# Steady attention chunks: the choice of the experts ahead of layer 2's first recurrence in VectorE's order

## The reference, cut to what matters

```python
def _time_mix_layer(x, ln_w, ln_b, Wk, Wv, Wr, Wo):
    normed = _layer_norm(x, ln_w, ln_b)
    k = einsum(normed, Wk); v = einsum(normed, Wv); r = sigmoid(einsum(normed, Wr))
    kv = k * v
    state = 0.95 * state + 0.05 * kv_t        # a scan over time
    return x + einsum(r * states, Wo)
x = layernorm(x + two_layers(x))
gate_out = einsum(x, Wg)
top_v, top_i = top_k(gate_out, 2)
probs = softmax(top_v)
out = sum over e of expert_e(x) * sum(probs * (top_i == e))
x = layernorm(x + out)
```

## Time and profile before

| | |
|---|---|
| median of 3 runs | 1275.16 us (1272.74 to 1279.75) |
| the profiled execution | 1267.26 us, its span 1265.5 us |
| TensorE busy | 1106.2 us, 87% of the span |
| DVE busy | 926.1 us, 73% |
| POOL busy | 869.1 us, 69% |
| ACT busy | 658.4 us, 52% |
| mean granted TensorE clock | 0.953 |

### The profile page before, as it was taken

The page is one execution under the profiler, slowest core; times in us unless marked ns, Lnnn a source line. Parts: engine busy times, 40 slices in busy tenths (PEclk is TensorE's granted clock), DMA queues, the critical chain, the costliest instruction groups (busy, mean ns, idle before and its releaser), DMA issues. The chain is left out here.

```text
span 1265.5 us, 23767 instructions
## 1 busy us (share of the span) xinstructions
PE 1106.2 (87%) x7172; PEld 990.4 (78%) x7172; DVE 926.1 (73%) x1973; ACT 658.4 (52%) x1091; POOL 869.1 (69%) x696
## 2 busy tenths in 40 slices
PE   7899888888888988738999999999999999999910
PEld 6777777777677777636888888888899999999910
DVE  6687888878887888746766666666667888888737
ACT  4455455555555444425544554445555666666618
POOL 3455777777877777667567776667667777777634
PEclk9999999999999999959999999999999999999965
DMA  3011111111111010237556665566669898888659
GB/s 150 17 51 67 43 43 52 51 50 50 50 50 39 31 48 34 67 102 196 146 148 161 158 153 142 140 155 159 148 156 229 240 228 247 227 244 227 141 165 384
DMA packets 80662, 164.20 MB, mean 130 GB/s; under 512 B 27424, under 2 KB 45600, under 8 KB 80352
## 3 DMA queue, kind: packets, MB, share of 16 engines
q1 hardware_dynamic: 49248, 126.16, 31.6%
q0 software_dynamic: 31360, 37.38, 15.7%
HBM read 118.01 MB, written 45.49 MB: 129 GB/s over the span
## 5 line engine op out<-in xcount | busy, mean ns | idle before, releaser
L1163 POOL DMA_INDIRECT x_acc<-fy_sb,pair_out x142 | 285.5, 2011 | 149.0 <-DVE fy_sb L1264 80.2
L1319 PE MATMUL fring<-fxh,fw_hi 128*128 128x256 f32 (+1 forms) x816 | 264.9, 325 | 3.6 <-DVE fxl L1255 1.9
L1321 PE MATMUL fring<-fxh,fw_lo 128*128 128x256 f32 (+1 forms) x816 | 265.4, 325 | 0.0
L1320 PE MATMUL fring<-fxl,fw_hi 128*128 128x256 f32 (+1 forms) x816 | 264.9, 325 | 0.0
L1182 ACT ACTIVATE fw_hi<-w_raw 128x1024 fp32r<-128x1024 f32 x153 | 161.1, 1054 | 150.0 <-PE fy L1362 138.7
L1235 DVE TENSOR_TENSOR fw_lo<-w_raw,fw_hi 128x1024 fp32r<-128x1024 f32 x153 | 186.5, 1219 | 17.9 <-ACT fw_hi L1182 17.0
L88 POOL DMA_INDIRECT xg<-x_src,pair_in x142 | 159.0, 1120 | 43.3 <-issue 42.7
L78 POOL DMA_INDIRECT slot_list<-pairs,slot_u x128 | 148.3, 1159 | 47.3 <-issue 30.5
L1319 PEld LDWEIGHTS fring<-fxh,fw_hi 128*128 128x128 f32 x816 | 153.7, 188 | 17.2 <-issue 2.3
L1320 PEld LDWEIGHTS fring<-fxl,fw_hi 128*128 128x128 f32 x816 | 153.7, 188 | 13.4
L1321 PEld LDWEIGHTS fring<-fxh,fw_lo 128*128 128x128 f32 x816 | 153.8, 188 | 13.2
(11 more groups left out here) (148 smaller groups left out, 2330.0 us busy)
## 6 DMA issues: line engine op xcount, KB each, us to landing
w_raw<-w_ffn SPq DMA_DIRECT2D x153, 512.0 KB
x_in<-h SPq DMA_DIRECT2D x16, 512.0 KB, 3.3
x_src<-x SPq DMA_DIRECT2D x16, 512.0 KB
x_acc<-x SPq DMA_DIRECT2D x16, 512.0 KB
acc<-x_acc SPq DMA_DIRECT2D x16, 512.0 KB, 7.6
out<-o SPq DMA_DIRECT2D x16, 512.0 KB, 6.6
xg<-x_src,pair_in POOLq DMA_INDIRECT x142
x_acc<-fy_sb,pair_out POOLq DMA_INDIRECT x142
```

The costliest lines, as they stand in the source:

```text
L1163: nc.gpsimd.indirect_dma_start(x_acc, bass.IndirectOffsetOnAxis(pair_out[j][:, q, 0:1].bitcast(U32), 0), y[j][:, q, :], None, compute_op=A ...
L1319: nc.tensor.matmul(out, hi, rows_hi, start=dc == 0, stop=False)
L1320: nc.tensor.matmul(out, hi, rows_lo, start=False, stop=False)
L1321: last = nc.tensor.matmul(out, lo, rows_hi, start=False, stop=dc == DC - 1)
```

## The change

On DVE, `choose(s - 3)` is now issued ahead of `recur(1, s - 1, 0)` in every step but s = 16 (`CHUNKS`), which keeps its own order. In steps 1 and 2 there is no choice yet, and in 17 and 18 no layer 2, so the order differs in steps 3 to 15. No other engine's code is touched.

```diff
                         recur(1, s - 1, e, j)
                         gated(dve, 1, s - 1, e)
                         y_lo(dve, 1, s - 1, e)
-                elif layer2:
-                    recur(1, s - 1, 0, j)
                 if within(s, 3, CHUNKS + 2) and not at(s, CHUNKS):
                     choose(s - 3)
+                if layer2 and not at(s, CHUNKS):
+                    recur(1, s - 1, 0, j)
                 if within(s, 1, CHUNKS - 2):
                     x_lo(0, s + 1)
                 if within(s, 3, CHUNKS + 2):
```

## The result

| | before | after |
|---|---|---|
| median | 1273.44 us (22 runs, 1266.65 to 1282.92) | 1266.27 us (22 runs, 1261.48 to 1278.64) |
| ratio, 95% interval | | 0.9948 (0.9924 to 0.9973) |
| the profiled execution, its span | 1267.26 us, 1265.5 us | 1267.21 us, 1265.4 us |
| mean granted TensorE clock | 0.953 | 0.956 |

The change takes 6.6 us off by the ratio (0.0052 x 1273.44; the interval gives 3.4 to 9.7), where the prediction's sum was 13.1. The time lies inside the range, 1254 to 1279.

A forecast was written before the change was run, and what follows sets the result against it. The prediction took a cross-engine chain, closed by DVE from gates to `nm`, as the bound. It summed 12.1 us for eleven chunks plus 3.0 for the clock, less 1 for each end chunk: 13.1 off, 1262 us, range 1254 to 1279.

The forecast's parts named there:

- What bounds the kernel: Chunks 4 to 14: no engine is full; a chain across engines, through DVE from gates to `nm`, closes the loop.
- G to `nm`: Stretch from the gates' end to `nm` of the next residual: 14.79 us in chunk 9, forecast to fall to 13.55.
- the end chunks: Chunks 3 and 15, the first and last edited: forecast to lose 1 us each.
- The choice first, the recurrence second: DVE in chunk 9, laid out anew: choice ends at 307.9 instead of 311.6, recurrence's scan ends 2.0 us later.
- TensorE's wait for `picked`: TensorE's 2.33 us wait for the choice's last step in chunk 9: goes, counted at nothing except through the clock.
- 0.25 is beyond both: The `slot_u` cast, 0.25 us ahead of POOL's `yl`, was forecast to pass, exceeding leads of 0.18 and 0.11.
- two near meetings: Earlier traces: a cast 0.18 ahead of `y` took 0.17 us; one 0.11 ahead of `yl` took 1.43.
- its first rival: The `slot_u` cast is held until `yl` ends: 0.24 us gained in chunk 9, 3.8 off in all, 1271; chance 0.25.
- The clock: Six of the eleven chunks lose TensorE's lower clock behind the wait for `picked`: 0.5 us each, 3.0 in all.
- The clock as a rival: TensorE's longer wait for the normalized rows lowers its clock, costing 2.0 us a chunk: 11 slower, 1286; chance 0.13.
- The gain stopping at POOL: Rival: stretched list writes delay POOL's second `yl`, so the power waits for POOL: 5 us off, 1270; chance 0.12.

The follow-up runs named there:

- e1: The changed kernel with the slot numbers' sum written as whole numbers at once, so without the cast of `slot_u`: 1258.08 us, ratio 0.9848 to the kernel before.
- e2: The kernel before, with the slot sum written as whole numbers at once, so without the cast of `slot_u`: 1272.78 us, ratio 0.9974 to the kernel before.
- e4: The changed kernel with the second half of layer 1's `xl` issued behind `place`, so the `slot_u` cast comes sooner: 1266.22 us, ratio 0.9930 to the kernel before.
- e6: e1 with POOL's layer 2 order changed to both list writes, then `y`, then both `yl` last: 1248.54 us, ratio 0.9818 to the kernel before.
- e8: The changed kernel, `slot_u` cast kept, with POOL's layer 2 order write, write, `y`, `yl`, `yl`: 1251.09 us, ratio 0.9821 to the kernel before.
- e3: The changed kernel with both of POOL's list writes issued ahead of the first `yl` of layer 2: 1272.41 us, ratio 0.9981 to the kernel before.
- e7: e6 with the recurrence ahead of the choice again, undoing the change alone: 1271.21 us, ratio 0.9983 to the kernel before.

## Why the prediction was half right

**What bounds the kernel** was right: the stretch from G to `nm` fell by 7.0 us over the chunks 4 to 14, the end chunks lost 1.2, and the time fell by 6.6. In each of the other kernels too the sum lies inside the interval of the ratio, in e1, e2 and e4 at its end; in e6 it is 23.1 us and the ratio gives 23.1, in e8 20.6 and 22.8.

**The choice first, the recurrence second.** Each step is where the prediction put it, counted from G in chunk 9: `kv` at 2.2 (305.64 - 303.41; forecast 307.9 - 305.70), `y` at 4.5 (forecast 4.5), `xl` at 4.7 (4.6), the cast at 6.8 (6.7), `yl` at 7.0 (6.95). TensorE's wait for `picked` was counted at nothing, rightly: it is gone, and the chunk is shorter only by what G to `nm` and the clock gave.

**The step that failed is "0.25 is beyond both".** The cast came 0.20 ahead of `yl`, near enough to the forecast 0.25, but the rule drawn from two near meetings was wrong. I took the lead over `yl` for what decides, because a lead of 0.18 had passed and one of 0.11 had not the earlier trace rows. The lead doesn't decide. The passed one, in chunk 5, had POOL idle for 0.97 ahead of `y`, as its row says. The held one, in chunk 14, was 0.92 into a list write that `yl` followed at once; this is POOL's row ahead of it, in the kernel before:

```profile
477.41 1.00 POOL L78 DMA_INDIRECT slot_list<-pairs,slot_u  x1 [0.16 <-issue]
```

In the changed kernel, the chunks 3 and 15 show it again:

```profile
117.37 0.17 DVE L737 CAST slot_u<-slot_f 128x8 uint32<-128x8 f32 x1
...
503.64 0.17 DVE L737 CAST slot_u<-slot_f 128x8 uint32<-128x8 f32 x1
```

```profile
117.45 1.30 POOL L305 TENSOR_TENSOR yl<-y,yh 128x512 fp32r<-128x512 f32 x1 [0.80 <-ACT yh L409]
...
503.43 1.00 POOL L78 DMA_INDIRECT slot_list<-pairs,slot_u  x1 [0.16 <-issue]
```

In chunk 3 a lead of 0.08 is enough; there no list write precedes `yl`, which has waited 0.80 for `yh`. In chunk 15 the cast is 0.21 into the write and passes. The eleven held ones are 0.68 to 0.93 into it, with leads of 0.11 to 0.35. So the prediction measured the cast against the wrong instruction: the sum had no line for the write, though POOL's order named it. What the runs showed in place of the pass is a cast of 1.50 that ends with `yl`, and G to `nm` at 14.53 instead of 13.55.

Whether the place in the write decides, or something that goes with it, stays open. `yl` also reads ACT's `yh`, and in every one of these writes, here, in e4 and in chunk 14 before, `yh` ends 0.50 to 0.52 into the write. The casts that pass start 0.06 to 0.30 ahead of that end, the held ones 0.17 to 0.43 behind it; so it may be that `yl` was free to go when the cast came. No run parts the two, and neither fits all of the scans. One in chunk 15 of the kernel before starts 0.57 into a write that `yl` follows at once, 0.06 behind the end of `yh`, and runs free, and `yl` takes longer:

```profile
508.53 1.29 DVE L692 TENSOR_TENSOR_SCAN state<-decay,carry,kv 128x512 f32<-128x512 f32 x1
```

```profile
507.96 1.00 POOL L78 DMA_INDIRECT slot_list<-pairs,slot_u  x1 [0.15 <-issue]
509.00 1.89 POOL L305 TENSOR_TENSOR yl<-y,yh 128x512 fp32r<-128x512 f32 x1
```

In e3 scans at 0.28 to 0.61 into such a write, over 1 us behind the end of `yh`, are held, and the one at 0.23, as far behind, runs free.

The Trainium skill (SBUF — State Buffer, Who interferes with whom) says that issue order decides who keeps the shared ports. Read on recorded starts of the cast and `yl` alone, that rule lets every cast here pass, and eleven of thirteen disagree with it. The same page of the Trainium skill (SBUF: two separate sides) says that the descriptors of a DMA issued by GpSimd are written through that pair too; with the write counted as a holder the rule agrees with e3's casts at 0.67 to 0.73 into a write, which took 0.25 to 0.31 and ended with it. It doesn't give the casts that pass at up to 0.44 into one, nor that `yl` goes ahead of a cast that was recorded before it. That it is the descriptors which hold the cast, no run here shows.

**The size.** The quiet loop chunks 9, 10 and 13 gained 0.22 on average; the forecast had 1.24 and 0.95, its first rival 0.24. That rival, the cast held, is what happened, down to the ends of its rows (cast with `yl`, scan free). It gave 3.8 us in all, too little, because it used 0.25 for the chunks 4, 5 and 14 as well, outside the loop, and these gained 1.37, 0.98 and 0.87 (4 and 5 with the 0.5 of the clock in it), and because it took 2 for the end chunks, which lost 1.2. That the time fell inside the range is no merit of the forecast's mechanism: the range held its 1262 and this rival's 1271 alike, and the 6.6 measured is half of its 13.1.

**The clock** was sized right: the loop chunks that had lost it (7, 8, 11 and 12) gained 0.76 on average against the 0.22 of the others, so 0.54 where 0.5 was taken. The clock as a rival didn't come: the wait for the normalized rows grew to 1.73, and the granted clock stays at 1.00 in ten chunks; chunk 6 lost it instead. There it cost nothing: from gates' copy to gates' copy chunk 6 lasts 32.54, and chunk 8, at 1.00, 32.53. In e1 four of the eleven chunks have 0.95, and they too are no longer than the others (chunk 9 31.78; chunk 11, at 1.00, 31.80). So what the lower clock costs depends on the order: it was priced in the old one, where it slows the output product that `xr` waits for.

**The end chunks.** Chunk 15, forecast at 1.0, lost 1.0: gates' copy to the next output product 13.47 (511.11 - 497.64, from the rows below) against 12.48 (503.02 to 515.50) before.

```profile
497.64 0.19 DVE L705 COPY g<-out 128x32 f32<-128x32 f32 x1 [2.55 <-PE out L912]
```

```profile
511.11 0.55 PE L876 MATMUL ring<-w_hi,yh 128*128 128x256 f32 x1 [5.56 <-issue]
```

Chunk 3, forecast at 1.0 for a held cast, lost 0.2: there the cast passed and the scan was held, to 1.60.

**The gain stopping at POOL** didn't come: `rs`, the power, starts 0.24 behind `nm` in all of these chunks, as before (318.18 - 317.94).

## What to carry to other kernels

When instructions move on one engine, lay out again what stands beside each of them on the engine that it gets in the way of, and count its DMA issues too: an instruction that costs 0.17 alone can cost 1.50 where a list write and another POOL instruction follow each other with almost no gap. A rule from two near meetings needs the row ahead of both. And a hold that is taken away may move to the next instruction: e3 removed one and made a longer one, and only when POOL's instructions were moved clear of both (e8, e6) did the reorder pay its full 1.8%.

## What the runs showed of the hardware

- A cast of 128x8 that starts in the last third of an indirect list write (0.67 to 0.93 of 1.0 us) takes 1.42 to 1.68 where `yl` follows the write within 0.04, and 0.17 to 0.31 where a gap of 0.30 and a second write follow.
- A reduction of 128x64 into whole numbers, at 0.43 to 0.67 into such a write, takes 0.22 in all of the chunks 4 to 14 of e1.
- A scan of 128x512 that starts 0.54 into a write takes 1.29 where nothing follows the write for 0.9 (e8), and 2.84 where `yl` follows at once (e3). In chunk 15 of the kernel before, 0.57 into a write that `yl` follows at once, it takes 1.29: place and follower alone don't settle it.
- The lower granted clock (0.95 in the chunk's mean) behind a wait of 2.3 on TensorE cost 0.54 a chunk in the kernel before, and 1.0 in e7, both with the recurrence first; with the choice first, in the changed kernel's chunk 6 and in four chunks of e1, it cost nothing.
